# One product instead of two for the row of a convolution kernel, with its low parts moved by VectorE

## The chip, the cores and the metric

One NeuronCore of a Trainium2 chip. Five engines run their own instruction streams and meet only at semaphores: TensorE (PE, matrix products, with its weight loads shown apart as PEld), VectorE (DVE), ScalarE (ACT), GpSimd (POOL) and SyncE (SP, which here only issues DMAs). The metric is the time of one execution on the device in microseconds, the median of several runs; less is better. The profile is of one such execution.

## What is computed

A masked long convolution (an S4 layer's kernel K, built from 64 complex states for each head), then a mixture of 64 experts of rank 16, gated by the top 16 of 64 scores, and a residual. Cut to what matters:

```python
def _get_kernel(log_dt, C, log_A_real, A_imag, length):
    Cc = C[..., 0] + 1j * C[..., 1]
    dt = jnp.exp(log_dt)
    A = -jnp.exp(log_A_real) + 1j * A_imag
    dtA = A * dt[:, None]
    P = dtA[:, :, None] * jnp.arange(length, dtype=jnp.float32)
    Cs = Cc * (jnp.exp(dtA) - 1.0) / A
    return 2.0 * jnp.einsum('hn,hnl->hl', Cs, jnp.exp(P)).real
# u_m = u * mask; y = (causal convolution of u_m with K, + u_m * D) * mask
# scores = y @ Wr.T; the 16 best of 64, softmaxed, are the gates G
# h = einsum('nd,krd->nkr', y, A); out = einsum('nkr,kdr->nd', h * G, B)
# result = x + 2.0 * out
```

There are 64 batches, 64 heads and 1024 positions; every head is a row of positions that the convolution treats by itself, and every (batch, head) is a row of 1024 values that the experts treat by itself.

## The kernel before

**Tiles and steps.** A tile is two heads (HT = 2) with all 64 batches, 128 rows in all; there are 32 tiles. The convolution of a tile works in 8 chunks of 128 positions: within a chunk by a 128x128 Toeplitz matrix of K (`near`), from chunk to chunk by the state of the recurrence (`feed`, `states`, `from_states`). Everything of importance is multiplied in split form: a value is a high part that ScalarE rounds (`..._hi`) and a low part that VectorE gets by subtracting (`..._lo`), and TensorE adds three products (high by high, high by low, low by high).

**The pipeline.** Step t does on every engine, in an order written out by hand: the expert products of tile t (`up`, 72 matmuls, and the two halves of `down` for tile t-1, 24 each), the convolution of tile t+1 (`near`, `from_states`), and the preparation of tile t+2 (`kernel_row`, `feed`); tables of sines and decays are made for tile t+3. The steps 0 to 3 (3 is `LAGGED`) and the last three are written out; a hardware loop runs the steps t = 4 to 28, 25 of them. What stands behind a wait in an engine's stream waits with it.

**The row.** For each head the decayed and turned powers of its 64 states, 128 partitions (real and imaginary parts, 16 and 16 in every group of 32), times the state's coefficients, are `out_raw` (128 x 2 heads x 130 positions). ScalarE copies it, rounded, to `o_hi` (`high_out`, L398), VectorE subtracts to `o_lo` (`low_out`, L655). K of the tile is the sum of the real parts over the states, which `kernel_row` (L1165, L1166) does as two matmuls into one bank: the fixed operand `real` is 1 in the rows of real parts and 0 in the others, the moving operands are the first 128 positions of `o_hi` and then of `o_lo`, 2 x 128 = 256 columns each. ScalarE copies the row to `k_sb` (`copy_k`, L423), a DMA spreads it to the Toeplitz matrix `t_lo`, ScalarE and VectorE split it (`high_near` L427, `low_near` L683), and `near` (L1195 to L1197) uses it one step later.

**VectorE's stream in a step of the loop**, in order: `first_states` (L697) and six rounds of `states` (L708, L710, L715) with the choice of the experts between them; `low_near` (L683) and `low_z` (L720), for which `near` and `from_states` (L1205) of this step wait; the gated products (L926), `low_squares` (L945), `out_factors` (L646, L650), `mask_y` (L724), `low_out` (L655), `turn_squares` (L940), `low_y` (L738), `low_x` (L688), `low_moved_in` (L667); `arguments` (L623, L625), whose result ScalarE turns into sines (L387) and, behind them, decays (L393), each after loading another table; `add_rows` (L961) and `add_skip` (L679); `make_powers` (L635), which waits for those decays; `turn_powers` (L662), `add_rows`, `scale_of` (L953), and the loop's branch.

Of the kernel before, what the change touches and what calls it, by code (L numbers as in the profile page):

```python
# [5 lines left out]
P = 128  # L6
# [5 lines left out]
HT = P // B  # L12
# [19 lines left out]
EXACT = 2  # L32
# [18 lines left out]
def build(nc, xt, x, length, parameters, a_t, b_t, wr_t, out):  # L51
# [19 lines left out]
    with ExitStack() as ctx:  # L71
        def sb(name, shape, dt=F32, where=ctx):
            return where.enter_context(nc.sbuf_tensor(name, shape, dt))
# [39 lines left out]
        hg = sb("hg", [P, D])  # L113
        mask = sb("mask", [P, NC, B], BF16)
        ident = sb("ident", [P, P])
        real = sb("real", [P, P], F32R)

        top_a, top_b = sb("top_a", [P, 8]), sb("top_b", [P, 8])
# [14 lines left out]
        with ExitStack() as early:  # L133
# [21 lines left out]

        square_in = sb("square_in", [P, HT * P])

        conv_ps = [ps(f"conv_ps{i}", [P, NC * B]) for i in range(HT)]
        h_ps = ps("h_ps", [P, 2, HALF])
        turn_ps = ps("turn_ps", [P, 2, HALF])  # L160
# [30 lines left out]

        s_theta, s_whole, s_args, s_sine, s_decay, s_powers, s_other, s_raw = (
            sem(n) for n in ("s_theta", "s_whole", "s_args", "s_sine", "s_decay", "s_powers", "s_other", "s_raw"))
        s_ohi, s_olo, s_turned, s_inhi, s_inlo, s_kps, s_kcopy, s_kdone = (
            sem(n) for n in ("s_ohi", "s_olo", "s_turned", "s_inhi", "s_inlo", "s_kps", "s_kcopy", "s_kdone"))
        s_thi, s_tlo, s_xhi, s_xlo, s_near = (sem(n) for n in ("s_thi", "s_tlo", "s_xhi", "s_xlo", "s_near"))
        s_fed, s_first, s_swap, s_part, s_state, s_zhi, s_zlo = (
            sem(n) for n in ("s_fed", "s_first", "s_swap", "s_part", "s_state", "s_zhi", "s_zlo"))
# [164 lines left out]
        def _(act):  # L363
# [31 lines left out]
            def high_out(t):  # L395
                act.wait_ge(s_raw, HT * t + HT)
                act.wait_ge(s_conv, HT * t)
                act.activation(o_hi[:, :, :], out_raw[:, :, :], ACT.Copy).then_inc(s_ohi, 1)  # L398

            def high_moved_in(t):  # L400

# [191 lines left out]
        def _(dve):  # L593
# [25 lines left out]

            def arguments(t):  # L620

                dve.wait_ge(s_theta, 2 * HT * t + 2 * HT)
                dve.tensor_scalar(powers_tmp, args[:, :, :, :], ROUND, ROUND, ALU.add, ALU.subtract).then_inc(s_whole, 1)  # L623
                dve.wait_ge(s_whole, t + 1)
                dve.tensor_tensor(out=args[:, :, :, :], in0=args[:, :, :, :], in1=powers_tmp, op=ALU.subtract).then_inc(s_args, 1)  # L625
# [27 lines left out]
            def low_out(t):  # L653
                dve.wait_ge(s_ohi, t + 1 - EXACT)
                dve.tensor_tensor(out=o_lo[:, :, :], in0=out_raw[:, :, :], in1=o_hi[:, :, :].bitcast(F32), op=ALU.subtract).then_inc(s_olo, 1)  # L655

            def turn_powers(t):

# [95 lines left out]

            powers_tmp = turned[:, :, :, :]

            dve.wait_ge(s_iota, 3)
            dve.tensor_copy(pos_f[:, :], pos_i[:, :])
            dve.tensor_copy(grid[:, :], grid_i[:, :])
# [3 lines left out]
            dve.tensor_scalar(phase_own[:, :], odd[:, :], -0.25, 0.25, ALU.mult, ALU.add)  # L763
            link(dve.tensor_scalar(phase_other[:, :], odd[:, :], 0.25, None, ALU.mult))
            dve.tensor_scalar(real[:, :], phase_own[:, :].to_broadcast([P, P]), 4.0, None, ALU.mult)
            dve.wait_ge(s_minus, 2)
            dve.tensor_copy(minus[:, :], minus_f[:, :]).then_inc(s_minus, 1)
            dve.wait_ge(s_par, 16 * 8)
# [203 lines left out]
            def first_step():  # L972
                gate(0)
                gates_of(0)
                gate_part(0, 0)
                gate_part(0, 1)
                sum_gates()
                low_weights(MIDST[4])
                first_states(1)
                states(1, range(1, 2))  # L980
                add_skip(1)
                low_weights(MIDST[5])
                gate_part(0, 2)
                low_gated(0, 0)
                states(1, range(2, 4))
                low_gated(0, 1)
                states(1, range(4, FED))
                arguments(2)
                scale_of(0)
                add_rows(0, 0)  # L990
                make_powers(2)
                out_factors(2)
                for i in range(HT):
                    mask_y(1, i)
                low_out(2)
                low_in(2)
                low_x(2)
                arguments(3)
                add_skip(2)
                add_rows(0, 1)  # L1000

            def second_step():
                first_states(2)
                states(2, range(1, MIDDLE))
                gate(1)
                states(2, range(MIDDLE, FED))
                gates_of(1)
                gate_part(1, 0)
                low_up(0)
                low_near(2)  # L1010
                gate_part(1, 1)
                low_z(2)
                sum_gates()
                gate_part(1, 2)
                make_powers(3)
                out_factors(3)
                low_gated(1, 0)
                low_gated(1, 1)
                for i in range(HT):
                    mask_y(2, i)  # L1020
                low_out(3)
                low_in(3)
                low_up(1)
                for i in range(HT):
                    low_y(2, i)
                low_x(3)
                low_up(2)
                scale_of(1)
                add_rows(1, 0)
                add_skip(3)  # L1030
                add_rows(1, 1)

            def third_step():
                first_states(3)
                states(3, range(1, MIDDLE))
                gate(2)
                states(3, range(MIDDLE, FED))
                gates_of(2)
                gate_part(2, 0)
                gate_part(2, 1)  # L1040
                low_near(3)
                low_z(3)
                sum_gates()
                gate_part(2, 2)
                arguments(4)
                low_gated(2, 0)
                low_gated(2, 1)
                make_powers(4)
                out_factors(4)
                for i in range(HT):  # L1050
                    mask_y(3, i)
                low_out(4)
                for i in range(HT):
                    low_y(3, i)
                low_x(4)
                low_in(4)
                arguments(5)
                scale_of(2)
                add_rows(2, 0)
                add_skip(4)  # L1060

            def step(t, conv=True, prep=True, table=True):

                second = isinstance(t, int) and t == LAGGED
                if conv:
                    first_states(t + 1)
                    states(t + 1, range(1, MIDDLE))
                gate(t)
                if conv:
                    states(t + 1, range(MIDDLE, FED))  # L1070
                gates_of(t)
                if conv:
                    low_near(t + 1)
                    low_z(t + 1)
                sum_gates()
                if not second:

                    dve.wait_ge(s_squares, t - LAGGED)
                for n in range(len(H_PARTS)):
                    gate_part(t, n)  # L1080
                if not second:
                    low_squares(t - 1)
                if prep:
                    if second:
                        make_powers(t + 2)
                    out_factors(t + 2)
                if conv:
                    for i in range(HT):
                        mask_y(t + 1, i)
                if prep:  # L1090
                    low_out(t + 2)
                if conv:
                    if not second:
                        dve.wait_ge(s_glo, 2 * t)
                    turn_squares(t)
                    for i in range(HT):
                        low_y(t + 1, i)
                if prep:
                    low_x(t + 2)
                    if second:  # L1100
                        low_in(t + 2)
                    else:
                        low_moved_in(t + 2)
                if table:
                    arguments(t + 3)
                if not second:
                    add_rows(t - 1, 0)
                if prep:
                    add_skip(t + 2)
                if table:  # L1110
                    make_powers(t + 3)
                    turn_powers(t + 3)
                add_rows(t - 1, 1)
                if conv:
                    scale_of(t)
# [28 lines left out]
        def _(pe):  # L1144
# [16 lines left out]

            def kernel_row(t):

                pe.wait_ge(s_olo, t + 1 - EXACT)
                pe.matmul(k_ps, real[:, :], o_hi[:, :, 0:P], start=True, stop=False)  # L1165
                pe.matmul(k_ps, real[:, :], o_lo[:, :, 0:P], start=False, stop=True).then_inc(s_kps, 1)  # L1166

            def whole_row(t, target):
                pe.wait_ge(s_raw, HT * t + HT)
# [295 lines left out]
```

## Time and profile before

| | |
|---|---|
| median of 3 runs | 911.78 us (911.59 to 912.97) |
| the profiled execution | 912.11 us, of which its span is 910.3 us |
| TensorE busy | 888.9 us, 98% |
| VectorE busy | 738.4 us, 81% |
| ScalarE busy | 380.7 us, 42% |
| chain that ended last | PE 92%, DVE 4%, DMA 2%, ACT 1% |
| DMA | 99.85 MB, 110 GB/s |

The chain that ended last is followed backwards from the last instruction, at each step to what released it. A wait that the profile names is the idle time of an engine ahead of an instruction, put down to the instruction that released it; where two engines take turns a wait may be short and still set the pace. Times of single instructions overlap on VectorE by under 0.1 us where nothing stands between them, and those of matmuls overlap by more: the distance from start to start is what counts.

### The profile page before, as it was taken

How to read it: one execution, taken by the hardware profiler on the slowest of the kernel's cores; microseconds unless marked ns; L12 is line 12 of the kernel's file. 1: busy time of each engine (PE TensorE's matmuls, PEld its weight loads, DVE VectorE, ACT ScalarE, POOL GpSimd, SP SyncE). 2: the span in 40 equal slices, each digit the busy share in tenths (PEclk: the TensorE clock that was granted, in tenths of full speed). 3: DMA queues.
4: the chain of work that ended last, by engine and by line, in shares of the span. 5: the costliest groups of instructions: out<-in, count | busy, mean ns of one | idle time of the engine just before them, and what ended most of it. 6: DMA issues, size and time to landing. Idle time of an engine off the chain costs nothing.

```text
span 910.3 us, 15546 instructions
## 1 busy us (share of the span) xinstructions
PE 888.9 (98%) x4536; PEld 791.5 (87%) x4536; DVE 738.4 (81%) x2473; ACT 380.7 (42%) x655; POOL 2.0 (0%) x12
## 2 busy tenths in 40 slices
PE   5999989999999999999999999999999999999998
PEld 4577978988999988899998899998889999889997
DVE  8899798888888888898888888888889888888722
ACT  4663344445334444434444533354443444442100
POOL 0000000000000000000000000000000000000000
PEclk9999999999999999999999999999999999999999
DMA  6631314443434443334443343444333444434331
GB/s 220 247 58 46 76 21 119 133 109 106 118 105 104 119 132 105 101 107 109 109 133 109 104 119 101 106 122 131 104 103 106 109 109 133 109 104 118 80 92 47
DMA packets 67123, 99.85 MB, mean 110 GB/s; under 512 B 22944, under 2 KB 49184, under 8 KB 67104
## 3 DMA queue, kind: packets, MB, share of 16 engines
q1 hardware_dynamic: 66400, 99.16, 39.8%
q10 hardware_dynamic: 704, 0.46, 0.2%
q8 instruction: 9, 0.15, 0.1%
q14 instruction: 10, 0.08, 0.0%
HBM read 60.52 MB, written 34.87 MB: 105 GB/s over the span
## 4 chain that ended last, share of the span: by engine, by line
PE 92%; DVE 4%; DMA 2%; ACT 1%; issue 1%; ACTq 0%; SPq 0%; DVEq 0%
PE out_ps L1239 25%; PE h_ps L1239 18%; PE out_ps L1243 12%; PE h_ps L1243 9%; PE turn_ps L1239 8%; PE turn_ps L1243 4%; PE conv_ps L1195 1%; PE conv_ps L1196 1%; PE conv_ps L1197 1%; PE h_ps L1248 1%; PE conv_ps L1178 1%; PE conv_ps L1179 1%; DMA b_in<-in_b_t 1%; PE conv_ps L1180 1%; PE conv_ps L1205 1%; PE conv_ps L1206 1%
## 5 line engine op out<-in xcount | busy, mean ns | idle before, releaser
L1239 PE MATMUL out_ps<-b_lo,g_hi 128*128 128x512 f32 x496 | 195.5, 394 | 0.0
L1239 PE MATMUL out_ps<-b_hi,g_hi 128*128 128x512 f32 x496 | 195.0, 393 | 0.0
L1239 PE MATMUL h_ps<-a_hi,y_hi 128*128 128x384 f32 x480 | 161.4, 336 | 0.0
L1239 PE MATMUL h_ps<-a_lo,y_hi 128*128 128x384 f32 x480 | 161.3, 336 | 0.0
L1243 PE MATMUL out_ps<-b_hi,g_lo 128*128 128x512 f32 x496 | 123.0, 390 | 0.0
L1243 PEld LDWEIGHTS out_ps<-b_hi,g_lo 128*128 128x128 f32 x496 | 93.1, 188 | 20.4
L1239 PEld LDWEIGHTS out_ps<-b_lo,g_hi 128*128 128x128 f32 x496 | 93.2, 188 | 19.6
L1239 PEld LDWEIGHTS out_ps<-b_hi,g_hi 128*128 128x128 f32 x496 | 93.2, 188 | 18.8
L715 DVE SCALAR_TENSOR_TENSOR z<-swapped,step_other,part 128x64 f32<-128x64 f32 x384 | 92.3, 281 | 12.0
L708 DVE SCALAR_TENSOR_TENSOR part<-z,step_own,conv_ps 128x64 f32<-128x64 f32 x384 | 90.3, 277 | 8.5
L1243 PE MATMUL h_ps<-a_hi,y_lo 128*128 128x384 f32 x480 | 93.1, 336 | 0.0
L1239 PEld LDWEIGHTS h_ps<-a_hi,y_hi 128*128 128x128 f32 x480 | 90.1, 188 | 0.0
L1239 PEld LDWEIGHTS h_ps<-a_lo,y_hi 128*128 128x128 f32 x480 | 90.1, 188 | 0.0
L1243 PEld LDWEIGHTS h_ps<-a_hi,y_lo 128*128 128x128 f32 x480 | 84.1, 188 | 0.0
L477 ACT ACTIVATE exp_all<-score_sb,neg_max 128x64 f32<-128x64 f32 x32 | 11.1, 348 | 147.9 <-DVE neg_max L903 147.9
L635 DVE TENSOR_TENSOR powers<-turned,decay 128x520 f32<-128x520 f32 x32 | 22.4, 699 | 61.5 <-ACT decay L393 60.8
L1239 PE MATMUL turn_ps<-a_hi,y_hi 128*128 128x320 f32 x240 | 71.6, 312 | 0.0
L1239 PE MATMUL turn_ps<-a_lo,y_hi 128*128 128x320 f32 x240 | 71.6, 312 | 0.0
L431 ACT ACTIVATE z_hi<-z 128x896 fp32r<-128x896 f32 x30 | 28.6, 953 | 87.8 <-DVE z L715 87.8
L398 ACT ACTIVATE o_hi<-out_raw 128x260 fp32r<-128x260 f32 x30 | 12.7, 422 | 124.9 <-DVE out_raw L650 119.5
L961 DVE SCALAR_TENSOR_TENSOR x_in<-out_ps,gate_scale,x_in 128x512 f32<-128x512 f32 x62 | 46.2, 745 | 15.2 <-PE out_ps L1243 15.0
L710 DVE STREAM_SHUFFLE swapped<-z 128x128 f32<-128x128 f32 x192 | 56.8, 296 | 0.0
(216 smaller groups left out, 1496.6 us busy)
## 6 DMA issues: line engine op xcount, KB each, us to landing
xt_in<-in_xt SPq DMA_DIRECT2D x32, 512.0 KB, 3.3
x_in<-in_x SPq DMA_DIRECT2D x62, 256.0 KB, 3.6
out<-x_in SPq DMA_DIRECT2D x62, 256.0 KB, 3.1
moved<-square_sb SPq DMA_DIRECT2D x28, 512.0 KB, 2.6
square_sb<-moved SPq DMA_DIRECT2D x112, 128.0 KB, 2.9
b_in<-in_b_t SPq DMA_DIRECT2D x8, 512.0 KB, 6.0
a_in<-in_a_t SPq DMA_DIRECT2D x8, 512.0 KB, 7.1
t_lo<-k_sb SPq DMA_DIRECT2D x62, 64.0 KB, 4.1
```

The source lines that it names most:

```text
L398: act.activation(o_hi[:, :, :], out_raw[:, :, :], ACT.Copy).then_inc(s_ohi, 1)
L431: act.activation(z_hi[:, :, :, :], z[:, :, :, :], ACT.Copy).then_inc(s_zhi, 1)
L477: act.activation(exp_all[:, :], score_sb[:, :], ACT.Exp, bias=neg_max[:, :]).then_inc(s_exp, 1)
L635: dve.tensor_tensor(out=powers[:, :, :, :], in0=turned[:, :, :, :], in1=decay[:, :, :].unsqueeze(2).to_broadcast([P, HT, 2, W]), op=ALU.mu ...
L708: dve.scalar_tensor_tensor(out=part[:, i, :], in0=z[:, c - 1, i, :], scalar=step_own[:, bass.ds(n + i, 1)], in1=conv_ps[i][:, c * B:(c + 1 ...
L710: dve.stream_shuffle(swapped[:, :, :], z[:, c - 1, :, :], SWAP).then_inc(s_swap, 1)
L715: dve.scalar_tensor_tensor(out=z[:, c, i, :], in0=swapped[:, i, :], scalar=step_other[:, bass.ds(n + i, 1)], in1=part[:, i, :], op0=ALU.mu ...
L961: dve.scalar_tensor_tensor(out=x_in[:, columns], in0=psum, scalar=gate_scale[:, :], in1=x_in[:, columns], op0=ALU.mult, op1=ALU.add).then_ ...
L1178: pe.matmul(fed, in_hi[:, i, :], xt_hi[:, i, 0:NS], start=True, stop=False)
L1179: pe.matmul(fed, in_hi[:, i, :], xt_lo[:, i, 0:NS], start=False, stop=False)
L1239: pe.matmul(o, hi[:, c, :], moving[:, c, columns], start=first and c == order[0] and moving is w_hi, stop=False)
L1243: last = pe.matmul(o, lo[:, c, :], w_hi[:, c, columns], start=False, stop=c == order[-1])
```

## The change

The low parts are moved across partitions and the row is one product. ScalarE, right behind `o_hi`, writes a second tile `row_in` with `out_raw` rounded in the rows of real parts and zero in the others (an activation with the per-partition scale `real_only`). VectorE, right behind `o_lo`, shuffles the low parts by 16 partitions within each group of 32, so that the low part of a real part lands on the partition of the imaginary part, and adds them, times `imaginary` (1 there, 0 elsewhere), to `row_in`. The fixed operand becomes all ones (once, in step 0), and one matmul of 256 columns sums high and low parts together. The shuffled values lie in the tile `turned`, so `arguments`, which writes there, waits for the row.

```diff
@@ ScalarE, high_out(t)
                 act.activation(o_hi[:, :, :], out_raw[:, :, :], ACT.Copy).then_inc(s_ohi, 1)
+                if not (isinstance(t, int) and t == EXACT):
+                    act.wait_ge(s_kps, t)
+                act.activation(row_in[:, :, :], out_raw[:, :, 0:P], ACT.Copy, scale=real_only[:, :]).then_inc(s_rhi, 1)
@@ VectorE
             def arguments(t):
+                if not (isinstance(t, int) and t <= EXACT):
+                    dve.wait_ge(s_row, t - EXACT)
...
+            def low_row(t):
+                dve.wait_ge(s_olo, t + 1 - EXACT)
+                dve.sem_inc(s_passed, 1)
+                dve.stream_shuffle(low_swapped, o_lo[:, :, 0:P].bitcast(F32), SWAP).then_inc(s_rswap, 1)
+                dve.wait_ge(s_rhi, t + 1 - EXACT)
+                dve.wait_ge(s_rswap, t + 1 - EXACT)
+                dve.scalar_tensor_tensor(out=row_in[:, :, :], in0=low_swapped, scalar=imaginary[:, :],
+                                         in1=row_in[:, :, :].bitcast(F32), op0=ALU.mult, op1=ALU.add).then_inc(s_row, 1)
...
+            low_swapped = turned[:, :, 0, 0:P]
...
+            dve.tensor_scalar(real_only[:, :], phase_own[:, :], 4.0, None, ALU.mult)
+            dve.tensor_copy(imaginary[:, :], odd[:, :])
@@ VectorE, first_step (and low_row(t + 2) behind low_out(t + 2) in every other step with a row)
                 low_out(2)
+                dve.wait_ge(s_kps, EXACT)
+                dve.tensor_scalar(real[:, :], phase_own[:, :].to_broadcast([P, P]), 0.0, 1.0, ALU.mult, ALU.add).then_inc(s_ones, 1)
+                low_row(2)
                 low_in(2)
@@ TensorE
             def kernel_row(t):
-                pe.wait_ge(s_olo, t + 1 - EXACT)
-                pe.matmul(k_ps, real[:, :], o_hi[:, :, 0:P], start=True, stop=False)
-                pe.matmul(k_ps, real[:, :], o_lo[:, :, 0:P], start=False, stop=True).then_inc(s_kps, 1)
+                if isinstance(t, int) and t == EXACT:
+                    pe.wait_ge(s_ones, 1)
+                pe.wait_ge(s_row, t + 1 - EXACT)
+                pe.matmul(k_ps, real[:, :], row_in[:, :, :], start=True, stop=True).then_inc(s_kps, 1)
```

VectorE's stream in the loop, before, from the low part of the output powers to the second use of `x_in`:

```order
424 L724 TENSOR_TENSOR y_m<-conv_ps,mask 128x8x64 x2
425 L655 TENSOR_TENSOR o_lo<-out_raw,o_hi 128x260
426 L940 STREAM_TRANSPOSE square_sb<-hg 128x1024
427 L738 TENSOR_TENSOR y_lo<-y_m,y_hi 128x8x64 x2
428 L688 TENSOR_TENSOR xt_lo<-xt_in,xt_hi 128x1024
```

The same place now:

```order
437 L747 TENSOR_TENSOR y_m<-conv_ps,mask 128x8x64 x2
438 L668 TENSOR_TENSOR o_lo<-out_raw,o_hi 128x260
439 L674 STREAM_SHUFFLE turned<-o_lo 128x2x128
440 L677 SCALAR_TENSOR_TENSOR row_in<-turned,imaginary,row_in 128x256
441 L967 STREAM_TRANSPOSE square_sb<-hg 128x1024
442 L761 TENSOR_TENSOR y_lo<-y_m,y_hi 128x8x64 x2
443 L711 TENSOR_TENSOR xt_lo<-xt_in,xt_hi 128x1024
```

Two instructions stand between `o_lo` and the transpose, and all that follows on VectorE follows them. ScalarE's stream in the loop has one more, now:

```order
131 L441 ACTIVATE z_hi<-z 128x896
132 L402 ISA
133 L404 ACTIVATE o_hi<-out_raw 128x260
134 L408 ACTIVATE row_in<-out_raw,real_only 128x256
135 L449 ISA
136 L450 ACTIVATE y_hi<-y_m 128x8x64
```

The copy with the scale stands ahead of `y_hi`. TensorE's stream has one matmul where there were two, at the same place between the two halves of `down`.

## Rows read from the trace of the kernel before

**Rows 1.** The page, busy us (share of the span) and instructions of each engine.

```profile
PE 888.9 (98%) x4536; PEld 791.5 (87%) x4536; DVE 738.4 (81%) x2473; ACT 380.7 (42%) x655; POOL 2.0 (0%) x12
```

**Rows 2.** Windows: busy us of each engine in one loop step, then PE clock, DMA.

```profile
400.93:427.85 26.92, 26.92 (x142) 24.47 (x140) 22.63 (x76) 11.65 (x20) 0.00 (x0) 1.00 0.41 112
```

**Rows 3.** Timeline of PE, a step of the loop: start us, duration us, instruction.

```profile
400.93 0.37 PE L1205 MATMUL conv_ps<-z_hi,o_hi 128*128 128x448 f32 x1
...
407.66 0.28 PE L1165 MATMUL h_ps<-o_hi,real 128*128 128x256 f32 x1
407.78 0.28 PE L1166 MATMUL h_ps<-o_lo,real 128*128 128x256 f32 x1
```

**Rows 4.** Timeline of DVE in the same step; in brackets idle time and its releaser.

```profile
404.24 0.42 DVE L655 TENSOR_TENSOR o_lo<-out_raw,o_hi 128x260 fp32r<-128x260 f32 x1
404.57 1.24 DVE L940 STREAM_TRANSPOSE square_sb<-hg 128x1024 f32<-128x1024 f32 x1
...
408.83 0.70 DVE L625 TENSOR_TENSOR args<-args,turned 128x520 f32<-128x520 f32 x1
...
412.49 0.70 DVE L635 TENSOR_TENSOR powers<-turned,decay 128x520 f32<-128x520 f32 x1 [2.22 <-ACT decay L393]
...
415.14 0.36 DVE L697 COPY z<-conv_ps 128x64 f32<-128x64 f32 x2 [0.52 <-PE conv_ps L1180]
...
425.54 1.09 DVE L720 TENSOR_TENSOR z_lo<-z,z_hi 128x896 fp32r<-128x896 f32 x1 [0.42 <-ACT z_hi L431]
```

**Rows 5.** Timeline of ACT in the same step.

```profile
408.50 1.28 ACT L387 ACT_TABLE_LOAD   x1
409.80 0.64 ACT L387 ACTIVATE turned<-args 128x520 f32<-128x520 f32 x1
```

**Rows 6.** Timeline of DVE: `arguments` in the loop's first and fourth step.

```profile
167.50 0.70 DVE L625 TENSOR_TENSOR args<-args,turned 128x520 f32<-128x520 f32 x1
...
247.42 0.70 DVE L625 TENSOR_TENSOR args<-args,turned 128x520 f32<-128x520 f32 x1
```

**Rows 7.** Timelines of DVE and of PE around the loop's first step.

```profile
157.29 1.09 DVE L720 TENSOR_TENSOR z_lo<-z,z_hi 128x896 fp32r<-128x896 f32 x1 [0.42 <-ACT z_hi L431]
...
173.56 0.35 DVE L697 COPY z<-conv_ps 128x64 f32<-128x64 f32 x2 [0.56 <-DVE gate_scale L953]
...
157.01 0.50 PE L1195 MATMUL conv_ps<-xt_hi,t_hi 128*128 128x512 f32 x1 [1.00 <-DVE t_lo L683]
```

**Rows 8.** Groups of DVE by form (busy us, mean ns), and one wait (us, times, longest).

```profile
L715 DVE SCALAR_TENSOR_TENSOR z<-swapped,step_other,part 128x64 f32<-128x64 f32 x384 | 92.3, 281 | 12.0
...
L710 DVE STREAM_SHUFFLE swapped<-z 128x128 f32<-128x128 f32 x192 | 56.8, 296 | 0.0
...
L650 DVE SCALAR_TENSOR_TENSOR out_raw<-powers,alpha,out_raw 128x130 f32<-128x130 f32 x64 | 19.8, 351 | 0.0
...
DVE top_b L907 <- DVE rest_a L904: 4.9, 31, 0.2
```

**Rows 9.** Timeline of PE in steps 0, 2 and 3, and two windows.

```profile
60.80 0.44 PE L1178 MATMUL conv_ps<-xt_hi,in_hi 128*128 128x448 f32 x1
...
115.21 0.38 PE L1165 MATMUL h_ps<-o_hi,real 128*128 128x256 f32 x1 [1.09 <-DVE o_lo L655]
...
118.08 0.47 PE L1178 MATMUL conv_ps<-xt_hi,in_hi 128*128 128x448 f32 x1 [2.37 <-DVE in_lo L674]
...
136.94 0.39 PE L1165 MATMUL h_ps<-o_hi,real 128*128 128x256 f32 x1 [1.02 <-DVE o_lo L655]
...
119.00:121.00 2.00, 2.00 (x9) 1.87 (x8) 1.92 (x10) 1.85 (x2) 0.00 (x0) 0.50 0.03 8
...
158.00:160.00 2.00, 2.00 (x11) 1.62 (x10) 2.00 (x6) 0.00 (x0) 0.00 (x0) 1.00 0.10 18
```

**Rows 10.** Timelines of DVE and of PE in the first step behind the loop.

```profile
829.25 1.09 DVE L720 TENSOR_TENSOR z_lo<-z,z_hi 128x896 fp32r<-128x896 f32 x1 [0.41 <-ACT z_hi L431]
...
831.65 0.37 PE L1205 MATMUL conv_ps<-z_hi,o_hi 128*128 128x448 f32 x1
```

More of the change, by code:

```diff
@@ L156, in build @@
         square_in = sb("square_in", [P, HT * P])
+        row_in = sb("row_in", [P, HT, P], F32R)
+        imaginary = sb("imaginary", [P, 1])
+        real_only = sb("real_only", [P, 1])
         conv_ps = [ps(f"conv_ps{i}", [P, NC * B]) for i in range(HT)]
@@ L193, in build @@
             sem(n) for n in ("s_theta", "s_whole", "s_args", "s_sine", "s_decay", "s_powers", "s_other", "s_raw"))
-        s_ohi, s_olo, s_turned, s_inhi, s_inlo, s_kps, s_kcopy, s_kdone = (
-            sem(n) for n in ("s_ohi", "s_olo", "s_turned", "s_inhi", "s_inlo", "s_kps", "s_kcopy", "s_kdone"))
+        s_rhi, s_rswap, s_row, s_ones, s_ohi, s_olo, s_turned, s_inhi, s_inlo, s_kps, s_kcopy, s_kdone = (
+            sem(n) for n in ("s_rhi", "s_rswap", "s_row", "s_ones", "s_ohi", "s_olo", "s_turned", "s_inhi", "s_inlo", "s_kps", "s_kcopy", "s_kdone"))
         s_thi, s_tlo, s_xhi, s_xlo, s_near = (sem(n) for n in ("s_thi", "s_tlo", "s_xhi", "s_xlo", "s_near"))
@@ L1021, in second_step @@
                 low_out(3)
+                low_row(3)
                 low_in(3)
@@ L1052, in third_step @@
                 low_out(4)
+                low_row(4)
                 for i in range(HT):
@@ L1091, in step @@
                     low_out(t + 2)
+                    low_row(t + 2)
                 if conv:
```

## The prediction

> **What bounds the kernel now.** I read the shares of the engines first: TensorE is busy 98% of the span, VectorE 81% [rows 1]. One step of the loop, from one `from_states` to the next, is 26.92 us, and TensorE has no gap in it [rows 2]. So at first sight TensorE alone sets the pace, and a matmul less is time less.
>
> The second reading is how near VectorE is. Its stream in a step of the loop, from one `z` copy to the next, runs through without a wait for TensorE; it waits for itself, for the branch, and for ScalarE on work that it has handed over itself. Two waits look otherwise and have to be read with care. The 0.52 us ahead of the `z` copy is put down to TensorE [rows 4]; but in the loop's first step, where VectorE is late and the profile names its own `gate_scale`, the same gap is 0.56 us [rows 7]. It is the cost of the loop's branch. The 2.22 us ahead of `powers` [rows 4] are ScalarE's sines, table load and decays, and these start when `args` is ready, 408.83 + 0.70 = 409.53, or when the table is loaded, 408.50 + 1.28 = 409.78; they start at 409.80 [rows 4, 5]. So in the steady loop ScalarE, which got there by way of TensorE's row, holds VectorE back by only some 0.25 us.
>
> The same number comes out of a view that needs no such reasoning. At the loop's start VectorE is behind, and TensorE waits 1.00 us for `t_lo` [rows 7]. From there VectorE goes at its own pace: its `args` start at 167.50 and, three steps later, at 247.42 [rows 6], 79.92 / 3 = **26.64 us a step**. After that it has caught up and goes at TensorE's 26.92. VectorE's own cycle is 0.28 us shorter than TensorE's, 1%, though its busy time is 22.63 of 26.92 us [rows 2]: the rest is latency inside its own chain and can't be filled by instructions that stand in its stream.
>
> **The change, part by part.** *TensorE* loses one matmul of 256 columns for each row, 0.12 us from start to start (407.66 to 407.78) [rows 3], 30 rows: -3.6 us where TensorE sets the pace, and its step would be 26.80 us.
>
> *VectorE* gets a shuffle and a scalar_tensor_tensor of 256 elements for each row, between `o_lo` and the transpose. The trace has the shuffle at 128 elements, 296 ns, and the other at 64 and 130, 281 and 351 ns, 1.06 ns for an element [rows 8]. I take 0.43 us for the shuffle (296 + 128 x 1.06) and 0.48 us for the other (351 + 126 x 1.06). Each needs the result of the one ahead of it. The first wait has a semaphore instruction behind it, as the one between `rest_a` and `top_b` has, which takes 4.9 / 31 = 0.16 us [rows 8]; the second has none, and I take 0.05, between nothing and 0.16. Before, the transpose starts 0.33 us after `o_lo`, 0.09 before its end [rows 4]. Now it starts 0.42 + 0.16 + 0.43 + 0.05 + 0.48 - 0.09 = 1.45 us after it. **VectorE's chain grows by D = 1.12 us a row.** Bounds: 0.97 with both waits at nearly nothing (0.03 each), 1.28 with 0.16 for both and 0.05 for the register work ahead of `arguments`' new wait.
>
> Here a rule of the Trainium skill speaks for less (VectorE: DVE Perf Modes, The DRAIN you can't avoid): a semaphore behind every Vector instruction costs nothing over none, count instructions, not waits. The row with 0.16 us between `rest_a` and `top_b` doesn't agree; the rule's result is the second rival.
>
> *ScalarE* gets an activation of 256 elements ahead of `y_hi`, some 0.4 us; it is busy 11.65 of 26.92 us [rows 2], and VectorE, 1.1 us later itself, needs `y_hi` no earlier than before. Nothing. *The new waits*: TensorE's row is needed at 407.66 and was ready at 404.66; it is ready about 1.1 us later, still 1.9 ahead [rows 3, 4]. The DMAs behind `k_sb`, `moved` and `x_in` start about 1.1 us later and are used more than half a step on. Nothing. The all-ones operand is one instruction, 0.1 to 0.3 us, once.
>
> *The loop.* VectorE's cycle becomes 26.64 + 1.12 = 27.76 us against TensorE's 26.80. VectorE sets the pace; TensorE waits about 0.95 us in every step, ahead of `near` for `t_lo`, as it does now only once [rows 7].
>
> *The sum.* I follow `z_lo`, behind which `from_states` starts. (1) Ahead of the loop three steps hand D on in full, because TensorE already stands waiting there for VectorE, or starts as the data comes: the `feed` of step 0 at 60.80, the row of step 2 at 115.21, the row of step 3 at 136.94 [rows 9]: 3 x 1.12, with the ones and less three matmuls, +3.3 us. (2) Between `z_lo` at 157.29 and `z_lo` at 829.25 [rows 7, 10] are 25 cycles, now 671.96 us, then 25 x 27.76 = 694.0: +22.0. (3) At the end of it `z_lo` is ready at 829.25 + 1.09 = 830.34, and TensorE uses it at 831.65 [rows 10]; this lead, less 0.13 for the hand-over, goes first: -1.2. (4) Behind it the streams have no tables, VectorE has time, and one matmul is saved: -0.1. Together 3.3 + 22.0 - 1.2 - 0.1 = **+24.0 us**. The profiled execution took 912.11 us, 1.8 more than its span, and lies 0.3 above the median of the runs; so 936.1 by it and **935.8** against the median. In the bounds of D, at 28 us for each us of D: 931.6 to 940.3.
>
> **The rivals.** *First, the gain* (the one that is not slower). VectorE is idle 4.3 of 26.92 us [rows 2], and 1.1 us would fit in there; then TensorE's saving is all: 912.1 - 3.6 = 908.5, less 0.3: 908.2. Its mechanism is that the 2.22 us ahead of `powers` are a cushion which ends at a fixed time set by TensorE's row. For it: `turned` starts right behind the table load. Against it: `args` ends only 0.25 us ahead of that. It decides at D = 26.80 - 26.64 = 0.16 us, and D is seven times as much.
> The Trainium skill (Perfetto Trace Analysis, Identifying the Most-Contended Engine) would have one look at the occupancy, which for VectorE is called a fair measure of the distance to its limit, and work on the most occupied engine first. By that this change is well aimed, and the time would be this rival's. The catching-up at 26.64 us a step says otherwise.
> *Second, dependent instructions overlap as free ones do.* If both new instructions hide 0.08 us and the waits cost nothing, D is (0.43 - 0.08) + (0.48 - 0.08) = 0.75, and the sum is 28 x 0.37 = 10.4 less: 925.4. Against it is the 0.16 us row.
> *Third, TensorE's clock falls.* Behind the waits of 1.09 and 2.37 us the granted clock was 0.50, that is 1.2 GHz, at 119 to 121 us [rows 9]; behind the 1.00 us at 157.01 [rows 7] it stayed at 1.00, 2.4 GHz [rows 9]. The waits of steps 2 and 3 grow by D, so a longer slow stretch there may cost 1 to 2 us. If the 0.95 us in every loop step brought it too, TensorE, with half-speed stretches of some 3 us that cost 1.7, would need 28.5 us in such steps; alternating with free ones, about 8 us more than forecast, 944.
>
> **Chances.** Forecast 0.80, the gain 0.09, free waits 0.05, the clock 0.04; that the change leaves no trace that can be measured, 0.02. The range is the bounds of D, with 2 us above for the clock of steps 2 and 3, and down to the second rival, without which it would hold too little: 925 to 942. A measurement of this kernel tells 0.2% from nothing: faster 0.09, same 0.02, slower 0.89.
>
> **What would show it.** `args` from start to start in the loop: 27.8 us if right, 26.8 if the gain is real. TensorE waits for `t_lo` some 0.9 to 1.0 us in nearly each loop step, over 20 us in all, and its busy share falls to 96% or less. From `o_lo` to the transpose 1.45 us. ScalarE's `turned` waits for `args` in all steps. The matmul of the row once, not twice, with no wait ahead of it in the loop. The prediction is wrong if VectorE waits anywhere in the loop for TensorE, or if the 2.22 us ahead of `powers` shrink by more than 0.3.

## The result and the profile after

The changed kernel took 939.15 us, the median of 4 runs (938.74 to 940.85). The kernel before, run beside it, took 912.35 us. The ratio is 1.0296, 95% interval 1.0283 to 1.0309: about 27 us slower, where 24.0 were forecast. The profiled execution took 940.85 us, of which its span is 939.1 us. Against the span of before, 910.3, that is +28.8 us, and this is the number that the terms below have to fill. The profiled execution is 1.7 us above the median of its own kernel; between the medians the difference is 26.8.

The page of the kernel after, busy us, share of the span and instructions of each engine (before: [rows 1]):

```profile
PE 895.5 (95%) x4506; PEld 786.0 (84%) x4506; DVE 765.2 (81%) x2566; ACT 387.5 (41%) x685; POOL 2.0 (0%) x12
```

TensorE has 30 instructions less and falls from 98% to 95%. VectorE's share is 81% as before, since the span has grown with it. The share alone would not say that VectorE now sets the pace; the chain that ended last does, on the same page:

```profile
DVE 54%; issue 18%; PE 17%; ACT 5%; DMA 3%; DVEq 2%; ACTq 1%; SPq 0%
```

It was 92% PE before. The waits of the kernel after, those that concern the change (engine, line, releaser; us in total, times, longest us):

```profile
ACT turned L393 <- DVE args L638: 68.4, 31, 4.7
...
PE conv_ps L1230 <- DVE t_lo L706: 19.8, 26, 1.1
...
PEld conv_ps L1240 <- DVE z_lo L743: 5.4, 26, 0.3
...
DVE turned L674 <- DVE o_lo L668: 4.8, 29, 0.2
PE h_ps L1201 <- DVE row_in L677: 4.5, 2, 2.3
...
PE conv_ps L1213 <- DVE in_lo L697: 2.3, 1, 2.3
```

TensorE waits 26 times for `t_lo`, as often as the loop has steps and once more. ScalarE waits for `args` 31 times; before it did so 9 times, 12.8 us in all. The row itself is waited for twice only, ahead of the loop. VectorE's timeline in a loop step of the kernel after, from the low part to `powers` (before: [rows 4]):

```profile
418.80 0.42 DVE L668 TENSOR_TENSOR o_lo<-out_raw,o_hi 128x260 fp32r<-128x260 f32 x1
419.38 0.01 DVE L674 LOAD_MASK_SELECT turned<-o_lo  x1 [0.17 <-DVE o_lo L668]
419.41 0.45 DVE L674 STREAM_SHUFFLE turned<-o_lo 128x256 f32<-128x256 f32 x1
419.97 0.48 DVE L677 SCALAR_TENSOR_TENSOR row_in<-turned,imaginary,row_in 128x256 fp32r<-128x256 f32 x1
420.37 1.24 DVE L967 STREAM_TRANSPOSE square_sb<-hg 128x1024 f32<-128x1024 f32 x1
...
424.63 0.70 DVE L638 TENSOR_TENSOR args<-args,turned 128x520 f32<-128x520 f32 x1
...
428.05 0.70 DVE L648 TENSOR_TENSOR powers<-turned,decay 128x520 f32<-128x520 f32 x1 [1.99 <-ACT decay L399]
...
452.49 0.70 DVE L638 TENSOR_TENSOR args<-args,turned 128x520 f32<-128x520 f32 x1
```

From `o_lo` to the transpose are 420.37 - 418.80 = 1.57 us, where [rows 4] have 0.33: D is 1.24 us. From `args` to `args` are 27.86 us. The idle time ahead of `powers` went from 2.22 to 1.99 and no further: it is ScalarE's own work on `args`, which starts when `args` is there, as ScalarE's and TensorE's timelines of the same step show:

```profile
421.96 1.28 ACT L393 ACT_TABLE_LOAD   x1
425.36 0.64 ACT L393 ACTIVATE turned<-args 128x520 f32<-128x520 f32 x1 [2.11 <-DVE args L638]
...
412.91 0.49 PE L1230 MATMUL conv_ps<-xt_hi,t_hi 128*128 128x512 f32 x1 [0.76 <-DVE t_lo L706]
...
421.24 0.28 PE L1201 MATMUL h_ps<-row_in,real 128*128 128x256 f32 x1
```

The table is loaded at 423.24 and ScalarE stands for 2.11 us until `args` ends. The row's matmul has no wait ahead of it.

### The profile page after: what moved, and what is told of

Same layout as the page of the kernel before. It is cut to its first block, busy times and chain, and to the rows that moved or that the text cites. A ratio compares the mean times of both kernels' runs of the same rounds, so it can differ in the third digit from the quotient of the medians.

```text
span 939.1 us, 15674 instructions
## 1 busy us (share of the span) xinstructions
PE 895.5 (95%) x4506; PEld 786.0 (84%) x4506; DVE 765.2 (81%) x2566; ACT 387.5 (41%) x685; POOL 2.0 (0%) x12
## 4 chain that ended last, share of the span: by engine, by line
DVE 54%; issue 18%; PE 17%; ACT 5%; DMA 3%; DVEq 2%; ACTq 1%; SPq 0%
DVE z L738 7%; DVE swapped L733 5%; DVE part L731 5%; PE out_ps L1274 4%; DVE y_m L747 4%; DVE hg L953 3%; DVE y_lo L761 3%; DVE xt_lo L711 3%; DVE g_lo L972 3%; ACT z_hi L441 3%; DVE powers L648 2%; DVE x_in L988 2%; PE out_ps L1278 2%; PE h_ps L1274 2%; DVE args L638 2%
```

## The experiments

The theory: VectorE's stream is a cycle of its own, 26.64 us a step, and what is put into it is paid once more than 0.28 us a step is put in. The rivals: its idle time takes the new work (the gain), TensorE's clock, and the operand, the copy on ScalarE or the new waits as causes.

**high_only**: the change without VectorE's part, so that the row lacks its low parts.

```diff
@@ against the kernel after
-                low_row(2)
...
-                    low_row(t + 2)
...
-                pe.wait_ge(s_row, t + 1 - EXACT)
+                pe.wait_ge(s_rhi, t + 1 - EXACT)
```

> The changed kernel without VectorE's two instructions for the row: no shuffle, no sum; the row is the one product of the high parts that ScalarE copies (the low parts of the row are left out). Theory (VectorE's chain sets the pace, its cycle is 26.64 us plus what is put into it): the chain is short again and TensorE's step is 26.80 us, so 30 x 0.12 us come off the kernel before: 908.7 us. Rival (the loss comes from ScalarE's copy or from the new order on TensorE): it stays near 939 us.

Measured 909.8 us, ratio 0.9969 (0.9958 to 0.9981). `args` in two steps that follow each other, timeline of DVE:

```profile
409.02 0.70 DVE L635 TENSOR_TENSOR args<-args,turned 128x520 f32<-128x520 f32 x1
...
435.80 0.70 DVE L635 TENSOR_TENSOR args<-args,turned 128x520 f32<-128x520 f32 x1
```

26.78 us a step where the forecast had 26.80 for TensorE with one matmul less. The saving is real, about 2.6 us of the 3.6. ScalarE's copy, the ones and TensorE's one matmul are in this kernel too, so all that makes the kernel slower is in the two instructions on VectorE or in the wait in `arguments`, which is left out here with them; own_tile, below, moves that wait away and keeps the two. At the loop's start VectorE is further behind here than in the kernel before, and its own cycle shows for eight steps: 26.63 to 26.67 us.

**work_two_products**: all of the new work on VectorE and ScalarE in every step, but TensorE forms the row as before (so the ones, once in step 0, are left out).

```diff
@@ against the kernel after
-                pe.matmul(k_ps, real[:, :], row_in[:, :, :], start=True, stop=True).then_inc(s_kps, 1)
+                pe.matmul(k_ps, real[:, :], o_hi[:, :, 0:P], start=True, stop=False)
+                pe.matmul(k_ps, real[:, :], o_lo[:, :, 0:P], start=False, stop=True).then_inc(s_kps, 1)
```

> All of the new work on ScalarE and VectorE, with TensorE waiting for it, but the row is made of the two products of the kernel before. Theory: TensorE waits about 1 us in each loop step anyway, so the second matmul costs nothing there: 939.4 us, 27.86 us a loop step, and TensorE's wait ahead of near is 0.12 us shorter. Rival (the saved matmul is worth its 3.6 us and other work costs 30): 942.8 us.

Measured 940.08 us, ratio 1.0299 (1.0281 to 1.0316), the kernel after within its interval. The wait in question:

```profile
PE conv_ps L1230 <- DVE t_lo L706: 16.8, 26, 1.0
```

It is 3.0 us less than the 19.8 of the kernel after: the second matmul takes 0.12 us a step out of TensorE's waiting and gives it to work. A matmul saved on an engine that waits is worth nothing, and here that can be read in one number.

**act_copy_only**: the kernel before with only ScalarE's copy added.

> The kernel before with ScalarE's copy into row_in alone (0.49 us ahead of y_hi, its result unused). Theory: ScalarE has room, nobody waits for it: 912.4 us, within 0.2%. Rival (the copy delays y_hi and with it VectorE's y_lo): up to 0.4 us a step, 10 us, 922 us.

Measured 912.66 us, ratio 1.0001 (0.9991 to 1.001). The copy of 0.49 us costs nothing.

**own_tile**: the shuffled values in the space of `swapped` and `part` in place of `turned`, so that `arguments` waits for nothing new; the wait for the row stands ahead of `first_states` instead.

```diff
@@ against the kernel after
             def arguments(t):
-                if not (isinstance(t, int) and t <= EXACT):
-                    dve.wait_ge(s_row, t - EXACT)
@@ first_states(t)
+                if not (isinstance(t, int) and t < EXACT):
+                    dve.wait_ge(s_row, t + 1 - EXACT)
```

> The changed kernel with the shuffled values in a tile of their own (over swapped and part) instead of in the one that arguments writes, so that arguments no longer waits for the row. Theory: that wait is already over when it is reached, so 939.2 us, 27.86 us a step. Rival (the wait through the shared tile is what lengthens the chain): 27.7 us a step or less and 935 us or less.

Measured 941.73 us, ratio 1.0319 (1.0302 to 1.0336), 1.6 us more than work_two_products, measured beside it, and 2.6 more than the kernel after. It misses what I expected, and most of the miss comes from the place to which the wait was moved: `first_states` is the first thing in the loop. The `z` copy there:

```profile
402.21 0.35 DVE L720 COPY z<-conv_ps 128x64 f32<-128x64 f32 x2 [0.58 <-DVE gate_scale L980]
```

In the kernel after this gap is 0.52 us. The 0.06 us, 25 times, are 1.5 us. So the wait in `arguments` had not cost anything: without it a step is 27.93 us (`args` at 396.13 and 424.06), the 27.86 of the kernel after and the 0.06 of the loop's head. A wait for something long done was not free at the head of the loop.

**fill_copy1, fill_stt1, fill_stt2** measure VectorE's slack directly. They are the kernel before with one or two instructions added on VectorE that belong to nothing: a copy of 64 elements (187 ns), or the scalar_tensor_tensor of 256 elements (478 ns) once or twice (the second in `arguments`).

```diff
@@ low_out(t), each of the three in its form
+                dve.tensor_copy(fill_out[:, 0:B], fill_in[:, 0:1].to_broadcast([P, B]))
...
+                dve.scalar_tensor_tensor(out=fill_out[:, :], in0=fill_in[:, 0:1].to_broadcast([P, HT * P]), scalar=fill_in[:, 1:2],
+                                         in1=fill_in[:, 0:1].to_broadcast([P, HT * P]), op0=ALU.mult, op1=ALU.add)
```

> The kernel before, with one idle copy of 64 elements on VectorE behind each o_lo (0.14 us from start to start). Theory (VectorE's cycle is 26.64 + D, and nothing happens until it passes TensorE's 26.92): 26.78 us, still under it, so the loop keeps 26.92 us and only the rows ahead of it, where TensorE waits, cost 3 x 0.14: 912.8 us, the same within 0.2%. Rival (every 0.1 us on VectorE costs as much in each of 30 rows): 912.4 + 4.2 = 916.6 us.

> The kernel before, with one idle scalar_tensor_tensor of 256 elements on VectorE behind each o_lo (D = 0.40 us). Theory: 27.04 us a step, 0.12 over TensorE's; 28 D - 7.2 = +4.0 us: 916.4 us. Rivals: VectorE's idle time absorbs it, 912.4; or it counts in full in every row, 28 x 0.40 = 11.2, 923.6.

> As the one before, with a second such instruction in arguments (D = 0.80 us in all, at two places). Theory: 27.44 us a step, 28 D - 7.2 = +15.2 us: 927.6 us, whatever the place in the chain. Rival (only what stands ahead of the row or of the wait for the decays counts): the place would matter, 916 us if what stands in arguments is free.

Measured 913.03 us (ratio 1.0009, 1.0 to 1.0019), 915.99 us (1.0044, 1.0027 to 1.0061) and 926.7 us (1.016, 1.0143 to 1.0177). `args` in two steps that follow each other, timelines of DVE, first of fill_copy1:

```profile
408.85 0.70 DVE L626 TENSOR_TENSOR args<-args,turned 128x520 f32<-128x520 f32 x1
...
435.77 0.70 DVE L626 TENSOR_TENSOR args<-args,turned 128x520 f32<-128x520 f32 x1
```

Then of fill_stt1:

```profile
412.61 0.70 DVE L626 TENSOR_TENSOR args<-args,turned 128x520 f32<-128x520 f32 x1
...
439.64 0.70 DVE L626 TENSOR_TENSOR args<-args,turned 128x520 f32<-128x520 f32 x1
```

And of fill_stt2:

```profile
417.86 0.69 DVE L627 TENSOR_TENSOR args<-args,turned 128x520 f32<-128x520 f32 x1
...
445.30 0.69 DVE L627 TENSOR_TENSOR args<-args,turned 128x520 f32<-128x520 f32 x1
```

The steps are 26.92, 27.03 and 27.44 us (27.42 on average over the loop). Each scalar_tensor_tensor adds 0.39 us to VectorE's cycle (0.478 less the overlap of 0.09), and 26.64 + 0.39 = 27.03, 26.64 + 0.78 = 27.42. The copy adds 0.10 from start to start, which is under the slack of 0.28, and the step stays TensorE's; while VectorE still catches up at the loop's start, its steps there are 26.73 to 26.75 us, 0.1 above 26.64. The three points lie on the forecast's 26.64 us plus what was added. That the step begins to grow at 0.28 follows from this line; the runs themselves put it between 0.10 and 0.39.

**head_only and loop_only** split the change by steps: the one product only in steps 0 to 2 (rows 2 to 4), or only in step 3 and the loop.

```diff
+            def merged(t):
+                return HEAD if isinstance(t, int) and t <= LAGGED + 2 else LOOPED
@@ high_out's second copy, low_row
+                if not merged(t):
+                    return
```

> The change in the four rows ahead of the loop alone; in the loop the two products and no work for the row on VectorE. Theory: the loop step is 26.92 us again and VectorE catches up in it, but what TensorE waited ahead of it stays lost: 3 x 1.24 us and the longer stretch at 1.2 GHz, some 1.6, less 0.4 for the saved matmuls: +4.9, 917.3 us. Rival (the profile's early part is only shifted and comes back in the loop): 912.4 us.

> The change in the 26 rows of the loop and behind it alone; the four rows ahead of it as in the kernel before. Theory: 25 cycles of 27.86 instead of 26.88 on average, +24.9 us, less the lead of 1.2 us that goes first: +23.7, 936 us; with the part ahead of the loop, measured alone at +3.4, it makes up the whole +26.8. Rival (the loop's loss feeds on the start's): clearly under 933 us.

Measured 915.57 us (ratio 1.0038, 1.0024 to 1.0052) and 935.06 us (1.0242, 1.0227 to 1.0258). That is +3.4 and +22.8 against the kernel before of each batch, together 26.2 of the 26.8 us of the whole. I had expected +4.9 of head_only. Three times 1.24 less the three or four saved matmuls is 3.3, so the medians leave nothing for the clock that I had added. The profiled execution of head_only, 1.1 us above its median, has a span of 914.8, +4.5.

**late_row and late_loop** ask whether the loss can be avoided while the saving is kept: the two instructions are put behind `args` and the first use of `x_in`, into VectorE's idle time ahead of `powers`. The row's matmul moves behind the second half of `down`, ScalarE's `copy_k` behind its tables, VectorE's `add_skip`, which needs that copy, behind the second `add_rows`, and the loads into `t_lo` behind `send_powers` on SP. late_loop does so in the loop and keeps two products in steps 0 to 2; late_row has one product there too.

```diff
@@ VectorE, step, behind the first x_in
+                if prep and not second:
+                    low_row(t + 2)
@@ TensorE, step
                 down(t - 1, 1)
+                if prep and not second:
+                    kernel_row(t + 2)
```

> The change in all rows, but in the loop VectorE makes the row in the gap in which it waits for the decays (between add_rows and make_powers), TensorE multiplies it behind the second half of down, ScalarE copies it behind its tables, and the DMA for t_lo goes out behind that. Theory: the two instructions, 1.24 us, fit in the gap of some 2 us, VectorE's cycle is 26.7 us and TensorE's 26.80, so the loop gains 25 x 0.12 = 3.0 us against the loss of 3.4 ahead of it: 912.5 us. Rival (VectorE's load as such is the limit): near 939 us. Second rival (the row now comes too late for t_lo): TensorE waits ahead of near by more than 1 us a step, 935 us or more.

> The row in one product and in VectorE's gap, in the loop and behind it alone; the four rows ahead of the loop with two products as in the kernel before. Theory: only the gain is left, 26 x 0.12 = 3.1 us: 909.2 us, faster than both kernels. Rival (the late row makes a new wait): not under 912 us.

Measured 917.46 us (ratio 1.0052, 1.0037 to 1.0067) and 913.39 us (1.001, 1.0001 to 1.0019). Timeline of DVE in a loop step of late_loop:

```profile
409.24 0.70 DVE L647 TENSOR_TENSOR args<-args,turned 128x520 f32<-128x520 f32 x1
...
410.53 0.44 DVE L685 STREAM_SHUFFLE both<-o_lo 128x256 f32<-128x256 f32 x1
411.08 0.48 DVE L688 SCALAR_TENSOR_TENSOR row_in<-both,imaginary,row_in 128x256 fp32r<-128x256 f32 x1
412.66 0.70 DVE L657 TENSOR_TENSOR powers<-turned,decay 128x520 f32<-128x520 f32 x1 [1.10 <-ACT decay L406]
...
436.12 0.70 DVE L647 TENSOR_TENSOR args<-args,turned 128x520 f32<-128x520 f32 x1
```

The same two instructions now lie in the idle time, which shrinks from 2.22 to 1.10 us, and 21.7 of loop_only's 22.8 us are gone. It is the placement in the chain that costs, not the work. But the 3 us of the saved matmul did not come; I had expected 909.2 of late_loop and 912.5 of late_row. Behind the loop's first step TensorE has no wait in late_loop, and still its step is 26.98 us, not 26.79, and longer than the 26.92 of the kernel before. From one `from_states` to the next, timeline of PE:

```profile
401.20 0.37 PE L1266 MATMUL conv_ps<-z_hi,o_hi 128*128 128x448 f32 x1
...
428.18 0.37 PE L1266 MATMUL conv_ps<-z_hi,o_hi 128*128 128x448 f32 x1
```

The `args` of the same stretch are 26.88 us apart, but that is VectorE catching up: its own cycle. After 13 steps it has caught up and goes at TensorE's pace too (timeline of DVE):

```profile
732.59 0.70 DVE L647 TENSOR_TENSOR args<-args,turned 128x520 f32<-128x520 f32 x1
...
759.58 0.70 DVE L647 TENSOR_TENSOR args<-args,turned 128x520 f32<-128x520 f32 x1
```

So there are two misses. VectorE's own cycle is 26.87 to 26.89 us in this order, not the 26.7 that I had expected; of the 0.23 above 26.64, 0.17 stands ahead of `add_skip`, where VectorE now waits for ScalarE's later copy. And TensorE's step is 0.19 us longer than in high_only, which has one matmul for the row too. The place of that loss is mostly in the expert products `up` of h. The same eight matmuls of 384 columns, grouped into a row, in a loop step of the timeline of PE, first in high_only:

```profile
420.94 1.55 PE L1271 MATMUL h_ps<-a_hi,y_lo 128*128 128x384 f32 x8
```

And in late_loop, with the granted clock of the stretch (the column behind POOL) at 1.00, 2.4 GHz:

```profile
421.13 1.58 PE L1304 MATMUL h_ps<-a_hi,y_lo 128*128 128x384 f32 x8
...
418.00:422.00 4.00, 4.00 (x25) 4.00 (x24) 3.52 (x22) 1.01 (x3) 0.00 (x0) 1.00 0.67 175
```

Every one of these matmuls follows the last after 176 to 177 ns instead of 173. Over both passes of 24 of them that is 0.16 us a step, 4 us in 25 steps, more than the 3 us that the matmul had saved; another 0.02 us a step is lost in `feed`, whose matmuls follow each other after 204 ns instead of 201. late_row has the same 176 ns.

**late_high** asks what makes them slower: late_loop without the two instructions on VectorE, so that the row lacks its low parts in the loop.

> late_loop, with the row's shuffle and its scalar_tensor_tensor left out, so that the row lacks its low parts; every other instruction, and its place, is that of late_loop. In late_loop TensorE had no wait in the loop and one matmul less, and still took 26.88 us a step: 24 matmuls of 384 columns stand there 4.24 us after 4.07 (start to start 176 ns, in the kernel before and in high_only 173 ns), some 0.16 us a step and 4 us in all. If the later places of the row, of ScalarE's copy and of the transfer make the matmuls slower: 176 ns again, a step of 26.87, 912.5 to 913.5 us. If the two instructions on VectorE do: 173 ns, a step of 26.79, 909.5 us. No theory of mine says which of the two it is; equal chances.

Measured 913.9 us (ratio 1.0017, 1.0007 to 1.0027). Timeline of PE and of DVE:

```profile
421.68 1.58 PE L1301 MATMUL h_ps<-a_hi,y_lo 128*128 128x384 f32 x8
...
413.21 0.70 DVE L657 TENSOR_TENSOR powers<-turned,decay 128x520 f32<-128x520 f32 x1 [2.06 <-ACT decay L406]
```

The slow matmuls stay with the two instructions gone, and so do both cycles: TensorE's step is 26.98 us and VectorE's own 26.88. (The 26.88 in what was expected, called TensorE's step there, is VectorE's.) So both come with the new places, of the row's matmul, of the copy, of `add_skip` or of the loads, and not with VectorE's two instructions. Which of them, and how, no run separates; the last section has what points to one.

## Why the prediction was right, step by step

**VectorE's own cycle, 26.64 against 26.92 us: right, and shown.** It was read from three steps of catching up [rows 6] and carried the forecast. The fillers put 0.39 us an instruction on it and found it again within 0.02, and high_only shows it in eight steps. With D at 1.24 it gives 27.88 for the kernel after; measured are 27.86.

**The gain: wrong, as forecast.** The idle time ahead of `powers` gave 0.23 us and not more, which is the 0.25 us between the end of `args` and the end of the table load. The Trainium skill (Perfetto Trace Analysis, Identifying the Most-Contended Engine) calls occupancy a fair measure of VectorE's distance to its limit; here VectorE was at 81% with 1% of a step to spare, and is at 81% now that it is the limit.

**D, the term that was mis-sized.** I had 1.12 and it is 1.24, inside the bounds of 0.97 to 1.28. The shuffle took 0.45 for 0.43 (256 elements, mean 449 ns), the scalar_tensor_tensor 0.48 as forecast (484). The wait behind `o_lo` was 0.16 to 0.17, as the row of `top_b` had it [rows 8]. The wait behind the shuffle was the miss: no semaphore instruction stands there, I took 0.05, and it is 419.97 - 419.86 = 0.11. The select of the shuffle's mask adds 0.03 between the first wait and the shuffle. Together 0.02 + 0.06 + 0.03, and 0.01 of rounding. The second rival, D of 0.75, is out. It was the result of the Trainium skill's rule (VectorE: DVE Perf Modes, The DRAIN you can't avoid) that the semaphore costs nothing; for instructions that need each other's results this trace has 0.17 and 0.11 us instead of an overlap of 0.09.

**The sum**, in the two profiled spans. (1) The head: `z_lo` of step 4 starts at 162.39 for 157.29 [rows 7], +5.1 us where +3.3 was forecast. Three times 1.24 are 3.7. Another 0.5 stands there already at the `feed` of step 0, which starts at 62.51 for 60.80 [rows 9], +1.7; the rest, about 1 us, is the clock, below. (2) The loop: `z_lo` behind it starts at 859.25,

```profile
859.25 1.09 DVE L743 TENSOR_TENSOR z_lo<-z,z_hi 128x896 fp32r<-128x896 f32 x1 [0.41 <-ACT z_hi L441]
```

so 25 cycles take 696.86 us for 671.96, +24.9 where +22.0 was forecast; 25 x 0.12 = 3.0 is the missing part of D. (3) The lead: TensorE starts `from_states` at 860.40, 0.06 behind the end of `z_lo`, for 1.31 before: -1.25, forecast -1.2. (4) The end: 28.8 - 5.1 - 24.9 + 1.25 = 0.05, forecast -0.1. The forecast was 24.0 against 28.8 in the spans and 26.8 in the medians. For the medians the missing part of D is enough: 28 x 0.12 = 3.4 us more make 27.4.

**TensorE's waits: right in kind, a little small.** 19.8 us in 26 waits for `t_lo`, 0.76 each, and 5.4 us in 26 for `z_lo`, 0.2 each, which I had put into the one wait: together some 0.97 a step, forecast 0.95.

**The clock: in the head of some executions, none in the loop.** Behind the waits in step 2, which grew from 1.09 and 2.37 us [rows 9] to 2.31 and 2.29, these are the windows of the kernel after (the clock is the column behind POOL):

```profile
120.00:122.00 2.00, 1.13 (x3) 1.05 (x4) 1.93 (x6) 0.38 (x2) 0.00 (x0) 0.55 0.00 0
122.00:124.00 2.00, 2.00 (x7) 1.83 (x7) 1.40 (x6) 1.97 (x3) 0.00 (x0) 0.50 0.01 4
124.00:126.00 2.00, 2.00 (x10) 2.00 (x9) 1.76 (x11) 2.00 (x6) 0.00 (x0) 0.50 0.60 26
126.00:128.00 2.00, 2.00 (x12) 2.00 (x12) 1.54 (x8) 0.11 (x1) 0.00 (x0) 0.74 0.34 48
```

and of the kernel before:

```profile
118.00:120.00 2.00, 1.92 (x7) 1.73 (x8) 1.93 (x7) 1.13 (x3) 0.00 (x0) 0.69 0.03 8
120.00:122.00 2.00, 2.00 (x9) 2.00 (x8) 1.82 (x11) 1.99 (x4) 0.00 (x0) 0.50 0.22 11
122.00:124.00 2.00, 2.00 (x14) 2.00 (x14) 1.76 (x11) 1.32 (x4) 0.00 (x0) 0.96 0.61 45
```

At 1.2 GHz TensorE worked from about 118.8 to 122.2 before, 3.4 us, and from 120.9 to 127.0 after, 6.1 us; 2.7 us more at half speed are up to 1.4 us lost. But the longer stretch does not follow from D alone. own_tile has the same two waits, 2.31 and 2.29 us, and these windows:

```profile
120.00:122.00 2.00, 1.40 (x4) 1.27 (x5) 1.93 (x6) 0.38 (x2) 0.00 (x0) 0.68 0.00 0
122.00:124.00 2.00, 2.00 (x8) 1.87 (x7) 1.46 (x8) 1.97 (x4) 0.00 (x0) 0.50 0.08 9
124.00:126.00 2.00, 2.00 (x15) 2.00 (x15) 1.76 (x9) 1.86 (x6) 0.00 (x0) 0.97 0.63 31
```

That is 3.4 us at 1.2 GHz, as before, and a second such stretch behind the wait of step 3. Its `z_lo` of step 4 starts at 161.16, +3.9 us; that of work_two_products, with 6.8 us at 1.2 GHz, at 161.45, +4.2. high_only, with no work for the row on VectorE, has 6.8 us too. So about 1 us of the head's +5.1 belongs to this one execution. The forecast named "1 to 2 us" for the clock in the rival, widened the range by it and left it out of the sum. The waits had to grow by D in any case, and the forecast has no reason for leaving it out; that the medians don't show it was luck. In the loop the waits of 0.76 us leave the clock at 1.00, so the third rival's part on the loop is out.

**The small ones.** ScalarE's copy, nothing: shown by act_copy_only. The wait in `arguments`, nothing: own_tile took it away, and beside the loop's head no step changed. The saved matmuls, worth nothing here: shown by work_two_products. That they would be worth 0.12 us a step with TensorE ahead: shown by high_only.

## What to carry to other kernels

Ask of the engine that is second how long its own cycle is, not how busy it is: a stretch in which it catches up after a late start shows it directly, and here 81% busy meant 1% of slack. Work that is moved from the bounding engine onto such a one costs its full length beyond that slack, with 0.1 to 0.2 us for each wait on the instruction ahead, unless it is put where the stream stands for another engine's answer: the same two instructions cost some 23 us in the loop behind `o_lo`, and nothing that could be measured ahead of `powers` (late_loop against late_high). And what such a move promises must be measured again, for the saved matmul's 3 us were lost to another effect. To see what a loop's step is, take it on the engine that sets the pace, or late in the loop: `args` of late_loop are 26.88 us apart for 13 steps while TensorE's step is 26.98.

## What was not expected of the hardware

The same matmuls go at two paces at the same granted clock. In the kernel before the products `up` of step 3 have the slower one, those of step 4, the loop's first, and of all later steps the faster (timeline of PE, step 3, then step 4):

```profile
131.52 1.58 PE L1243 MATMUL h_ps<-a_hi,y_lo 128*128 128x384 f32 x8
...
150.29 1.55 PE L1243 MATMUL h_ps<-a_hi,y_lo 128*128 128x384 f32 x8
```

It holds through the whole section of 48 matmuls, while in the loop those of 320 columns ahead of it keep their 146 to 147 ns. late_row, late_loop and late_high have the slower pace in `up` of the steps 5 to 30, each of which follows a step with the row at its late place; in step 4, which follows the row of step 3 at its old place, and in step 31, which follows a step without a row, they have the faster. `up` of step 3 goes at the slower pace in 5 of the 14 profiled kernels. Common to all the slow ones is that the row's matmul stood right ahead of `feed` in the step before, as it always does in step 2; where it stood between the halves of `down`, the pace was the faster in every profile. That points to the row's place in TensorE's stream, but in the loop `copy_k`, `add_skip` and the loads moved with it, and in step 3 the same place gave both paces. What sets the pace was not found.

The waits of step 2 don't tell how long TensorE stays at 1.2 GHz behind them. Waits of 1.09 and 2.37 us were followed by 3.4 us at that clock (the kernel before), 1.09 and 2.56 by 6.8 (fill_stt1), 2.31 and 2.29 by 6.8 (the kernel after) and by 3.4 (own_tile). Waits of 0.76 us once a step had no such effect.

A wait on VectorE for a semaphore long set was free in the middle of the stream (in `arguments`) and cost 0.06 us at the loop's head (own_tile), where the branch is.
